# A state-space loop that spreads C first in each turn, with 16-expert gates and code-book loads moved

## The reference, cut to what matters

```python
# layer 0, feed-forward: 16 experts (8 of width 128, 8 of width 256), the 8 best per token
probs = softmax(x @ router.T);  topk_w, topk_idx = top_k(probs, 8)
topk_w = topk_w / topk_w.sum(-1);  comb[token, topk_idx] = topk_w
for e in range(16):
    out += comb[:, e:e+1] * (gelu(x @ w1[:, off:off+wd]) @ w2[off:off+wd, :])

# layer 1: state-space block, forwards and on the flipped sequence, 384 channels, 16 states
u = silu(causal_conv(x @ in_w));  dt, B, C = split(u @ xproj_w)
delta = softplus(dt @ dt_w + dt_b)
h_t = exp(delta_t * A) * h_(t-1) + (delta_t * u_t) * B_t      # a scan for each state n
y_t = sum over n of h_t[n] * C_t[n]  + u * D;  out = (y * silu(z)) @ out_w

# layer 2, feed-forward: 8 subspaces, 64 codes each, the 4 best codes per token and subspace
z = x @ P;  scores = z . C;  w = softmax(top_k(scores, 4))
h = gelu(z @ W1[code] + b1[code]);  out = gelu((sum of w * (h @ W2[code] + b2[code])) @ G1) @ G2
```

## Time and profile before

| | us |
|---|---|
| median of 3 runs | 3295.45 (3294.97 to 3295.58) |
| the profiled execution | 3295.63 |
| its span | 3293.8 |
| PE busy | 2360.9 (72%) |
| DVE busy | 2278.2 (69%) |
| ACT busy | 1592.2 (48%) |
| POOL busy | 1046.5 (32%) |
| 16-expert stage, first product to the end of the stage | 222.28 to 494.56 |
| state-space loop, first scan to the last | 572.4 to 1271.3 |
| opening of the code-book stage | 2054.33 to 2118.6 |

### The profile page before, as it was taken

How to read it: one execution, slowest core, us unless ns; L and a number is a source line. 1 busy time by engine, 2 the same in 40 slices (tenths; PEclk the granted TensorE clock), 3 DMA queues, 4 the chain that set the end, 5 groups by cost and what they waited for, 6 DMA issues and landing times. The chain is left out here.

```text
span 3293.8 us, 39013 instructions
## 1 busy us (share of the span) xinstructions
PE 2360.9 (72%) x12580; PEld 1429.7 (43%) x12620; DVE 2278.2 (69%) x5846; ACT 1592.2 (48%) x2954; POOL 1046.5 (32%) x578
## 2 busy tenths in 40 slices
PE   5859994888888876799821112788889788773456
PEld 4646662334334334599611112322222466663345
DVE  5753334898989996211379996688888699997521
ACT  3221113667675652111217773677778556655111
POOL 2000002888898983577100000000000033443032
PEclk9969996899999998899955555899999899997578
DMA  2230002222222223311100000344435400000321
GB/s 55 37 118 1 1 0 98 78 103 103 78 103 92 96 96 87 117 41 40 58 0 0 0 1 15 116 129 142 147 122 186 131 1 1 1 1 1 129 79 57
DMA packets 86535, 219.13 MB, mean 67 GB/s; under 512 B 35709, under 2 KB 53339, under 8 KB 76891
## 3 DMA queue, kind: packets, MB, share of 16 engines
q1 hardware_dynamic: 80188, 204.38, 18.4%
q0 software_dynamic: 6144, 12.25, 1.2%
HBM read 199.46 MB, written 25.03 MB: 68 GB/s over the span
## 5 line engine op out<-in xcount | busy, mean ns | idle before, releaser
L2467 DVE TENSOR_TENSOR_SCAN mam_st<-mam_da,mam_st 128x512 f32<-128x512 f32 x384 | 441.1, 1204 | 39.4 <-ACT mam_da L2407 35.7
L2235 POOL TENSOR_TENSOR mam_st<-mam_du,mam_b_rows 128x1536 f32<-128x1536 f32 x128 | 442.4, 3457 | 79.7 <-PE mam_ysum L2305 55.7
L2305 PE MATMUL mam_ysum<-mam_st,held_ident 128*128 128x512 f32 x768 | 366.0, 615 | 0.0
L1863 ACT ACTIVATE cod_hp<-cod_up,cod_b 128x512 f32<-128x512 f32 x512 | 316.7, 703 | 83.5 <-PE cod_up L1724 83.3
L2407 ACT ACTIVATE mam_da<-mam_delta,mamw_decay 128x508 f32<-128x508 f32 x384 | 251.6, 681 | 177.6 <-DVE mam_st L2467 142.2
L2606 POOL TENSOR_TENSOR att_probs<-att_se,att_neg 128x1536 f32<-128x1536 f32 x16 | 55.0, 3440 | 811.2 <-DVE att_neg L2816 811.2
L2305 PEld LDWEIGHTS mam_ysum<-mam_st,held_ident 128*128 128x128 f32 x768 | 151.2, 199 | 153.7 <-issue 150.3
L692 DVE SCALAR_TENSOR_TENSOR held_h<-x_dn,held_gate,held_h 128x192 f32<-128x192 f32 x256 | 89.1, 411 | 182.6 <-PE x_dn L659 180.9
L2816 DVE MATCH_REPLACE8 att_neg<-att_top,att_neg 128x128 f32<-128x128 f32 x768 | 201.1, 276 | 0.3 <-issue 0.3
L2005 DVE TENSOR_TENSOR cod_hp<-cod_hp,cod_gate 128x512 f32<-128x512 f32 x256 | 164.0, 683 | 46.4 <-ACT cod_hp L1863 45.9
L1724 PE MATMUL cod_up<-cod_zr,cod_w1r 96*128 96x512 bf16 x512 | 180.2, 391 | 15.6 <-ACT cod_hp L1863 9.3
(11 more groups left out here) (552 smaller groups left out, 5366.0 us busy)
## 6 DMA issues: line engine op xcount, KB each, us to landing
cod_wide_gates<-gate_scratch SPq DMA_DIRECT2D x128, 512.0 KB, 3.9
mam_b_rows<-b_scratch SPq DMA_DIRECT2D x32, 1024.0 KB, 6.8
mam_c_rows<-b_scratch SPq DMA_DIRECT2D x32, 1024.0 KB, 4.7
slot_scratch<-in_slot_fresh SPq DMA_DIRECT2D x2, 3860.0 KB, 14.3
sw_w<-in_L_w SPq DMA_DIRECT2D x1, 6144.0 KB, 18.5
grw_w<-in_L_w SPq DMA_DIRECT2D x1, 5376.0 KB, 42.7
grw_w<-in_L_w SPq DMA_DIRECT2D x1, 4608.0 KB
sw_w<-in_L_w SPq DMA_DIRECT2D x1, 4608.0 KB, 31.4
```

Of the source, the lines that this page charges most:

```text
L1863: nc.scalar.activation(hp[step % HOLD][:, j, :], up[u % BANKS][:], ACT.Gelu_apprx_tanh, bias=b1[:, sub * HT + f:sub * HT + f + 1]).then_in ...
L2235: nc.gpsimd.tensor_tensor(st[it % N_ST][:], du[r % 2][:], along(b_rows[:, p % RING, n % PIECE, :], 1, [P, MC, MT]), ALU.mult)\
L2305: last = nc.tensor.matmul(ysum[:, c, :], m.ident[:], st[it % N_ST][:, c, :], start=False, stop=(it % DS == DS - 1))
L2467: nc.vector.tensor_tensor_scan(fs, fa, fs, 0.0, ALU.mult, ALU.add).then_inc(scanned, 1)
```

## The change

It has three parts.

1. *State-space loop.* `spread_c(it)` becomes the first product of a turn on PE; the small product comes behind it. All else stays.
2. *16-expert gates.* The norm ahead of the experts no longer computes gates. `experts_stage` does it: DVE's list there begins with the gates, ahead of its adds. PE begins with the ups of 12 pairs (`AHEAD`) and stays 12 pairs ahead; ACT has 28 tiles (`NHT`) for the gelu.
3. *Code-book loads.* A stage around norm and code-book stage holds the first weights and the tiles that `w1` is split in. The norm's SP issues five of the loads (w1 in two halves); DVE splits half 0 at the end of the norm (`tail`), and half 1 at the start of the code-book stage. PE waits for all loads only before the spreading of `z`, and for half 1 only before the second 16 groups.

```diff
@@ norm_stage
-               wide=None):
+               wide=None, tail=None):
...
+            if tail is not None:
+                tail(v)
@@ experts_stage
-def experts_stage(nc, m, a, name, tiles, func, w1_sb, w2_sb, w_in, wide):
-    E, NT, NUP, NHT = len(tiles), sum(tiles), 4, 4
+def experts_stage(nc, m, a, name, tiles, func, w1_sb, w2_sb, w_in, wide, gate):
+    E, NT, NUP, NHT = len(tiles), sum(tiles), 4, 28
+    AHEAD, HB = NT // 2, NB // 2
...
-            up_products(0, 0)
+            for i in range(AHEAD):
+                up_products(*pairs[i])
             for i, (g, p) in enumerate(pairs):
-                if i + 1 < len(pairs):
-                    up_products(*pairs[i + 1])
+                if i + AHEAD < len(pairs):
+                    up_products(*pairs[i + AHEAD])
                 for e in sorted({owner[2 * p], owner[2 * p + 1]}):
                     down_products(g, e)
...
         @block.vector
         def _(v):
+            c = Chain(v, dve)
+            c.step(nc.vector.memset(gate.work[:], 0.0))
+            for k in range(2):
+                gate.steps(nc, c, m, slice(k * HB, (k + 1) * HB))
@@ codes_stage
+def split_w1(nc, v, w, h):
+    x, part = w.w1[:, h], [p[:, h] for p in w.w1_part]
+    base = 3 * h
+    v.wait_ge(w.w1_in[h], 16)
+    nc.vector.tensor_copy(part[0], x).then_inc(w.split_own, 1)
+    v.wait_ge(w.split_own, base + 1)
+    nc.vector.tensor_tensor(x, x, part[0], ALU.subtract).then_inc(w.split_own, 1)
+    v.wait_ge(w.split_own, base + 2)
+    nc.vector.tensor_copy(part[1], x).then_inc(w.split_own, 1)
+    v.wait_ge(w.split_own, base + 3)
+    nc.vector.tensor_tensor(part[2], x, part[1], ALU.subtract).then_inc(w.w1_split, 1)
+
+def codes_stage(nc, m, a, w):
...
-            for dst, src in ((proj[:], "S_proj"), (codes[:], "S_codes")):
-                sp.dma_start(dst, a[src]).then_inc(p_in, 16)
-            sp.dma_start(w1, a["S_w1"]).then_inc(w1_in, 16)
-            for dst, src in ((sel_w[:].bitcast(I16), "sel_w"), (sel_z[:].bitcast(I16), "sel_z"),
+            for dst, src in ((sel_z[:].bitcast(I16), "sel_z"),
...
-            sp.wait_ge(w1_split, 1)
+            sp.wait_ge(w1_split, 2)
             send_gates(0)
...
-            pe.wait_ge(p_in, 32)
+            pe.wait_ge(p_in, 48)
             for h in range(2):
                 project(0, h, first_turn(h), first_ready)
             pe.wait_ge(first_kept, 2)
             for t in range(GS):
                 score(0, t, first_turn(2 + t), first_ready)
-            pe.wait_ge(w_in, 16 * N_IN)
             pe.wait_ge(w1_split, 1)
             for i in range(N_W // 2):
                 spread_w1(i, first_turn(first_w(i)))
+            pe.wait_ge(w_in, 16 * N_IN)
             for sub in range(SS):
                 spread_z(0, sub, first_turn(FIRST_ZR + sub), first_ready)
+            pe.wait_ge(w1_split, 2)
...
-            v.wait_ge(w1_in, 16)
-            own.step(nc.vector.tensor_copy(w1_part[0], w1))
-            own.step(nc.vector.tensor_tensor(w1, w1, w1_part[0], ALU.subtract))
-            own.step(nc.vector.tensor_copy(w1_part[1], w1))
-            nc.vector.tensor_tensor(w1_part[2], w1, w1_part[1], ALU.subtract).then_inc(w1_split, 1)
+            split_w1(nc, v, w, 1)
             rest_z(0)
@@ s_l2ffn
-    norm_stage(nc, m, a, "n5")
-    codes_stage(nc, m, a)
+    with Stage(nc, "codw") as s:
+        w = Loads()
...
+        norm_stage(nc, m, a, "n5", ahead=[
+            (w.w1[:, 0], a["S_w1"][:, 0], w.w1_in[0]), (w.proj[:], "S_proj", w.p_in), (w.codes[:], "S_codes", w.p_in),
+            (w.sel_w[:].bitcast(I16), "sel_w", w.p_in), (w.w1[:, 1], a["S_w1"][:, 1], w.w1_in[1])],
+            tail=lambda v: split_w1(nc, v, w, 0))
+        codes_stage(nc, m, a, w)
@@ mamba_stage, PE's list
                 for n in range(DS):
                     it = r * DS + n
+                    spread_c(it)
                     if r + 1 < ROUNDS_M:
                         late = 3 if odd else 0
...
-                    spread_c(it)
                     if n == LATE_SUM:
                         skips(r)
@@ s_l0ffn
-        norm_stage(nc, m, a, "n1", router="L0_router", n_routes=16, gate=Gate(16, 8, True), wide=wide,
+        norm_stage(nc, m, a, "n1", router="L0_router", n_routes=16, wide=wide,
...
-        experts_stage(nc, m, a, "x1", tiles, ACT.Gelu_apprx_tanh, w1_sb, w2_sb, w_in, wide)
+        experts_stage(nc, m, a, "x1", tiles, ACT.Gelu_apprx_tanh, w1_sb, w2_sb, w_in, wide, Gate(16, 8, True))
```

More of the change, by code:

```diff
@@ L629, in experts_stage @@
         dn_ready, dn_added = s.sem("dn_ready"), s.sem("dn_added")
+        dve = s.sem("dve")
+        gate.tiles(s, HB)
         block = s.block()
@@ L1541, in first_w @@
     return W1_AT + i + (SS if i >= N_W // 2 else 0)
-def codes_stage(nc, m, a):
+def split_w1(nc, v, w, h):
[10 more added lines that the diff above has]
+def codes_stage(nc, m, a, w):
     with Stage(nc, "cod") as s:
-        proj = s.sb("proj", [DC, 2, 2 * P])
-        codes = s.sb("codes", [P, 2, 4 * SM])
+        proj, codes, sel_w, wide_gates, hp = w.proj, w.codes, w.sel_w, w.wide_gates, w.hp
+        p_in, w1_split = w.p_in, w.w1_split
         sel_z = s.sb("sel_z", [P, 4, NPART, KR], BF16)
-        sel_w = s.sb("sel_w", [P, 4, NPART, KR], BF16)
         sel_g = s.sb("sel_g", [P, NBLK, P], BF16)
@@ L1561, in codes_stage @@
         turned_gates = s.sb("turned_gates", [P, 2, GT])
-        wide_gates = s.sb("wide_gates", [P, GRING, QD, GT])
-        hp = [s.sb(f"hp{i}", [P, QS, GT]) for i in range(HOLD)]
         ex = s.sb("ex", [P, GS * SS, SM])
@@ L1575, in codes_stage @@
         b2 = comb_t[:].rearrange("p h t -> p (h t)")[:, 0:2 * NSP * 32].rearrange("p (n r) -> p n r", r=32)
-        w1 = wide_gates[:].rearrange("p i j t -> p (i j t)")[:, 0:2 * SM * SH].rearrange("p (h f) -> p h f", h=2)
-        w1_part = [hp[i][:].rearrange("p j t -> p (j t)").bitcast(BF16).rearrange("p (h f) -> p h f", h=2)
-                   for i in range(NPART)]
+        w1_part = w.w1_part
         up = [s.psum(f"up{i}", [P, 512]) for i in range(BANKS)]
@@ L1583, in codes_stage @@
         first_bank = up + gate + [misc]
-        names = ("w_in p_in w1_in w1_split first_ready first_kept zeroed misc_ready misc_kept z_high z_low z_rest_ready z_mid "
+        names = ("w_in first_ready first_kept zeroed misc_ready misc_kept z_high z_low z_rest_ready z_mid "
                  "shifted exped weighted w_high w_rest w_mid w_low up_ready gate_ready h_ready gated downed "
                  "comb_kept b2_ready dve act_own").split()
-        (w_in, p_in, w1_in, w1_split, first_ready, first_kept, zeroed, misc_ready, misc_kept, z_high, z_low, z_rest_ready, z_mid,
+        (w_in, first_ready, first_kept, zeroed, misc_ready, misc_kept, z_high, z_low, z_rest_ready, z_mid,
          shifted, exped, weighted, w_high, w_rest, w_mid, w_low, up_ready, gate_ready, h_ready, gated, downed,
@@ L1591, in codes_stage @@
         gates_in = [s.sem(f"gates_in{i}") for i in range(GRING)]
-        N_IN = 10
+        N_IN = 9
         block = s.block()
@@ L2081, in s_l2ffn @@
 def s_l2ffn(nc, m, a):
-    norm_stage(nc, m, a, "n5")
-    codes_stage(nc, m, a)
+    with Stage(nc, "codw") as s:
+        w = Loads()
+        w.proj, w.codes = s.sb("proj", [DC, 2, 2 * P]), s.sb("codes", [P, 2, 4 * SM])
+        w.sel_w = s.sb("sel_w", [P, 4, NPART, KR], BF16)
+        w.wide_gates = s.sb("wide_gates", [P, GRING, QD, GT])
+        w.hp = [s.sb(f"hp{i}", [P, QS, GT]) for i in range(HOLD)]
+        w.w1 = w.wide_gates[:].rearrange("p i j t -> p (i j t)")[:, 0:2 * SM * SH].rearrange("p (h f) -> p h f", h=2)
+        w.w1_part = [x[:].rearrange("p j t -> p (j t)").bitcast(BF16).rearrange("p (h f) -> p h f", h=2) for x in w.hp]
+        w.p_in, w.split_own, w.w1_split = s.sem("p_in"), s.sem("split_own"), s.sem("w1_split")
+        w.w1_in = [s.sem(f"w1_in{h}") for h in range(2)]
+        norm_stage(nc, m, a, "n5", ahead=[
[3 more added lines that the diff above has]
+        codes_stage(nc, m, a, w)
 DI, DS, DT, TAPS = 2 * D, 16, 12, 4
```

## The result

The changed kernel takes 3280.04 us (median of 5 runs, 3274.8 to 3280.33), the kernel before beside it 3295.45: 0.9944 of it, 95% interval 0.9928 to 0.996. The forecast was 3279.2. Its profiled execution has a span of 3278.5 us, where that of before had 3293.8.

A forecast was written before the change was run, and what follows sets the result against it. PE bounds the experts' stage, DVE the loop with PE close behind; the code-book opening is a chain of waits. 10.7 - 15.4 - 11.7 = -16.4 us gives 3279.2 us; range 3274 to 3284, eight in ten 3264 to 3287.

The forecast's parts named there:

- Even rounds, conv: Loop, turns 1 to 3 of even rounds from round 2: late convolution product delays scan(4); +2.0 us a round.
- Rival (b): Loop: the edit does what it aims at, all 21.0 us of DVE's waits come off, 3247.5 us; chance 0.05.
- Even rounds, dt: Loop, turn 7 of even rounds: last dt product starts later, ACT's stretch comes 0.8 us later; +0.8 us.
- Outputs: Loop, turns 11 and 12 of rounds 2, 4, 6: spread no longer stands behind outputs; -1.2 us a round.
- Odd rounds: Loop, rounds 1, 3, 5: convolution 0.4 us later, 0.2 where exp and log follow later dt; +0.6 us each.
- Round 0: Loop, first round: convolution no longer hidden before the first scan, scan(4) moves 3.3 us; with the dt turn +4.1 us.
- (c): Loop: PE queues more, a conv phase's backlog reaches the next; loop +14 to +22, 3282.5 to 3290.5 us; chance 0.08.
- (d): Loop: waiting spread delays small products in each of 76 turns by 1.8 us; with half, 3337 us; chance 0.05.
- Gates: 16-expert stage: PE starts 17.4 us earlier with gates hidden behind up products, slower end costs 2.0; -15.4 us.
- The tail's 3.2 us a pair: End of experts' stage: four down pairs with two small experts, without ups, take 3.2 us each, not 2.7; +2.0 us.
- Loads: Code-book opening: PE starts 2.1 us earlier, spreading of z comes 12.3 us earlier, second exit costs 0.6; -11.7 us.
- The second exit: End of code-book stage: the added outer stage has another exit, 1.60 us against 1.0; +0.6 us.

The follow-up runs named there:

- e3: Changed kernel with the small product ahead of the spread again in turns 1 to 3 (convolution) of the even rounds; 3268.22 us.
- e10: Changed kernel with the small product (first convolution product) ahead of the spread again in turn 1 of the even rounds alone; 3271.62 us.
- e5: Changed kernel with the small product ahead of the spread again in turns 5 to 7 (dt) of the even rounds; 3269.52 us.
- e9: The changed kernel run again, unaltered; 3277.2 us.
- e2: The kernel before with only the new loop order, spread first; 3308.18 us.
- e7: Changed kernel with PE 8 pairs of up products ahead and not 12; 3278.16 us.
- e8: Changed kernel with both halves of w1 split at the start of the code-book stage, none in the norm; 3281.17 us.
- e4: Changed kernel with the spread first only in turns 11 and 12 (outputs) of rounds 2, 4 and 6, old order elsewhere; 3265.56 us.

## Why the prediction was right, step by step

- **Even rounds, conv: +2.0.** Measured 2.02, at each of the three points named, and 2.01 taken back in e3. Rival (b) fell with it. "From there PE has no gap in either order" holds for 1.65 of it (e10).
- **Even rounds, dt: +0.8.** Turns 7 and 8 of round 2 take 11.56 us together, 10.47 before: 1.09. Mis-sized by 0.3; putting dt back is worth 1.3 (e5).
- **Outputs: -1.2.** 14.77 to 13.51 us in turns 11 and 12 of round 2: -1.26.
- **Odd rounds: +0.6.** Measured 0.47 in rounds 3 and 5.
- **Round 0: +4.1.** Measured 4.57 and 4.38 (e9) with conv(1) at 6.39 and 6.27 us, 3.0 to 3.1 (e2, e7, e8) with conv(1) at 4.9 to 5.0. The price goes with the granted clock in conv(1): 0.56 and 0.57 there, 0.72 to 0.74 here. The prediction took 6.1 us for it; before has 6.28 at 0.57, with PE idle for 4.56 us ahead of the spread in front of it.
- **Mis-sized: the loop's clock.** The prediction let the granted clock be the same in both orders. By e2 its sum is off by 0.6, but by luck: round 0 is 1.0 and the odd rounds together 0.4 below it, the even rounds 1.2 and round 7 0.8 above. In the changed kernel it is off by 3.4, the most of it in turn 1 of round 1 (+1.9) and turn 3 of round 7 (+0.8), where it had counted next to nothing.
- **Rivals (c) and (d).** The loop ends at the lower edge of (c)'s 14 to 22 us, but not by its mechanism: no conv phase's backlog reaches the next round; rounds 3 and 5 pay 0.47. (d) falls: the prices are those of the turns named, not 1.8 us a turn.
- **Gates: -15.4.** Measured -15.34: -17.6 to PE's start (35.33 against 52.97 us from the norm's first instruction; forecast -17.4) and +2.3 behind it (forecast +2.0). The eight other profiles with 12 pairs ahead have -14.8 to -17.0, so the nearness is in part luck. The tail's 3.2 us a pair was 3.12. The first pair took 4.51 at a granted clock of 0.65, near the 4.48 of before, at 0.65 too, that the prediction's sum has: PE stood idle 1.02 us ahead of it and not 18.65, and in 196 to 204 us it had been busy 8.00 of 8 us at a granted clock of 0.50.
- **Loads: -11.7.** Measured -12.86. PE's start (20.9 us after the norm's) and the length of the 16 spreads (10.4) came as worked out; projections and scores took 10.4 us and not 11.4, at a granted clock of 0.76 against 0.71. The second exit cost 0.4 and not 0.6: DVE is idle 1.37 us before the next norm, 0.95 before. Beside POOL's memset the first cast of DVE's second half took 4.55 us, and that of the first half 1.22; in e8_no_tail, where the first half runs beside the memset, it is that one which takes 4.55 and the other 1.22. Nobody waited for it in the changed kernel: DVE stood 2.62 us for ACT's exp behind it.

## What to carry to other kernels

A wait that is removed is worth what ends next behind it: look for the engine that stands a few instructions on, and price the work that the edit puts behind a waiting instruction. An in-order queue is best ordered turn by turn: the spread belongs first where nothing urgent hangs on the product that it passes (the outputs), and last where a long chain does (the convolution, dt). When several parts go in together, measure them apart; here one part gave back half of what the two others brought (14.1 of 28.2 us).

## What the runs showed of the hardware that was not expected

- The same loop takes 704 or 707 us, by where the granted clock is low (changed kernel and e9_again 707.05 and 706.81, e7_eight and e8_no_tail 704.07 and 704.02). One product of it, the first convolution product of round 0, takes 6.39 us at a granted clock of 0.56 in the changed kernel and 4.92 at 0.73 in e7_eight.
- In the norm ahead of the experts the granted clock rose for a while in four of the profiles (e4, e5, e9, e10) and fell again under a busy PE. e9_again, columns as in the earlier trace rows:

```profile
184.00:186.00 2.00, 1.95 (x12) 1.40 (x10) 0.38 (x2) 1.96 (x5) 0.00 (x0) 0.70 1.01 433
186.00:188.00 2.00, 2.00 (x14) 1.83 (x15) 0.00 (x0) 1.81 (x6) 0.00 (x0) 1.00 0.13 45
...
190.00:192.00 2.00, 2.00 (x9) 1.85 (x9) 0.00 (x0) 0.67 (x2) 0.00 (x0) 0.50 0.00 0
192.00:203.20 11.20, 11.16 (x44) 10.27 (x44) 0.00 (x0) 2.11 (x6) 0.00 (x0) 0.50 0.00 0
```

  The norm then takes 32.85 us to PE's first up product and not 35.33, and the first pair behind it 5.3 to 5.6 us and not 4.5 to 5.1; norm and stage together take 308.3 to 308.6 us, elsewhere with 12 pairs ahead 309.9 to 310.5. A busy PE and a high granted clock did not go together there: PE was busy in 11.16 of 11.20 us at a granted clock of 0.50, some 4 us behind a stretch at 1.00 (186 to 188 us).
- Stretches that no part of the change touches differ by 2 to 4.5 us between executions: the start to the 16-expert norm took 169.3 to 172.9 us in these profiles, the norm behind the loop to the code-book norm 742.5 to 747.0. A change of a few us is better read from its own stage than from the whole time.
